# GpSimd splits three of the four blocks of each attention's output, and the projection takes them ahead of the last normalisation

## The reference

```python
xn = _ln(x, norm_s_w, norm_s_b)
spatial_out = _spatial_experts(xn, idx_s, sp_in_w, sp_in_b, sp_out_w, sp_out_b)
xt = _ln(x, norm_t_w, norm_t_b)
temporal_out = _temporal_experts(xt, idx_t, tq_w, tq_b, tk_w, tk_b, tv_w, tv_b, tp_w, tp_b)
fused = _cross_mha(spatial_out, temporal_out, cross_in_w, cross_in_b, cross_out_w, cross_out_b)
x = x + fused
h2 = _ln(x, norm_mlp_w, norm_mlp_b)
x = x + (jax.nn.gelu(h2 @ mlp_w1.T + mlp_b1, approximate=False) @ mlp_w2.T + mlp_b2)
```

## Time and profile before

| | us |
|---|---|
| median of 3 runs (lowest, highest) | 1732.79 (1730.02, 1736.64) |
| the profiled execution, its own time | 1727.27 |
| its span, first to last instruction | 1725.5 |
| PE busy | 1596.2 (93%) |
| DVE busy | 1148.8 (67%) |
| ACT busy | 879.1 (51%) |
| POOL busy | 734.6 (43%) |

### The profile page before, as it was taken

One profiled execution on the slowest core, in us unless ns is written; L12 is line 12 of the kernel. 1 busy time (PEld: TensorE's weight loads), 2 busy tenths in 40 slices (PEclk: granted clock), 3 DMA queues, 4 the chain that ended last, 5 costly groups with the idle time before them and its releaser, 6 DMA issues.

```text
span 1725.5 us, 26353 instructions
## 1 busy us (share of the span) xinstructions
PE 1596.2 (93%) x9714; PEld 1355.3 (79%) x9714; DVE 1148.8 (67%) x1810; ACT 879.1 (51%) x1733; POOL 734.6 (43%) x596
## 2 busy tenths in 40 slices
PE   2788999699999999999999998999999997899997
PEld 1567877588788888878789996878888885678876
DVE  7998826720788988840288885168888887843323
ACT  3795313320788878732177772158878873301100
POOL 3120222145446545033568744363546465532430
PEclk9999999799999999989999998999999998899999
DMA  3000021333111112042222304302111210110111
GB/s 105 13 26 2 26 66 46 111 147 72 23 39 31 31 31 61 2 184 69 60 60 61 73 7 156 85 1 52 40 31 31 55 66 19 37 38 25 49 36 59
DMA packets 37347, 91.62 MB, mean 53 GB/s; under 512 B 6457, under 2 KB 8975, under 8 KB 36712
## 3 DMA queue, kind: packets, MB, share of 16 engines
q1 hardware_dynamic: 37224, 89.99, 18.9%
HBM read 45.40 MB, written 13.86 MB: 34 GB/s over the span
## 4 chain that ended last, share of the span: by engine, by line
PE 78%; DVE 8%; ACT 5%; POOL 4%; issue 3%; DMA 2%; DVEq 1%; SPq 0%; POOLq 0%; ACTq 0%
PE ps L1000 12%; PE ps L730 12%; PE ps L731 11%; PE ps L732 11%; PE ps L981 11%; PE ps L966 7%; PE ps L967 6%; DMA w_raw<-in_weights 1%; PE ps L925 1%; PE ps L926 1%; POOL F L638 1%; PE ps L1016 1%; ACT F L1173 1%; ACT F L1260 1%; DVE F L1568 1%
## 5 line engine op out<-in xcount | busy, mean ns | idle before, releaser
L1186 ACT ACTIVATE R<-ps 125x500 fp32r<-125x500 f32 (+3 forms) x632 | 291.8, 508 | 147.0 <-PE ps L981 145.6
L583 POOL TENSOR_TENSOR w_hi<-w_raw,zero 128x512 fp32r<-128x512 f32 x92 | 110.5, 1201 | 593.0 <-PE ps L732 282.4
L1767 DVE TENSOR_REDUCE TB<-ps 125x1 f32<-125x1250 f32 (+4 forms) x240 | 299.5, 1263 | 82.9 <-PE ps L967 56.5
L1776 DVE TENSOR_TENSOR R<-ps,R 125x500 fp32r<-125x500 f32 (+3 forms) x632 | 324.1, 569 | 12.9 <-ACT R L1186 12.9
L1173 ACT ACTIVATE F<-ps,TB 125x1250 f32<-125x1250 f32 (+4 forms) x240 | 276.1, 1157 | 60.2 <-DVE TB L1767 60.2
L1000 PE MATMUL ps<-R 125*128 125x252 f32 (+1 forms) x2080 | 288.9, 286 | 2.3 <-DVE F L1819 2.3
L981 PE MATMUL ps<-ident,F 125*125 125x125 f32 x2040 | 260.1, 275 | 9.6 <-ACT F L1173 8.5
L1000 PEld LDWEIGHTS ps<-R 125*128 125x128 f32 x2080 | 256.0, 189 | 2.6 <-DVE R L1776 1.6
L981 PEld LDWEIGHTS ps<-ident,F 125*125 125x125 f32 x2040 | 239.8, 189 | 12.9 <-ACT F L1173 12.4
L966 PE MATMUL ps<-R 128*125 128x512 f32 (+5 forms) x624 | 240.5, 386 | 5.1 <-DVE R L1776 4.0
L730 PE MATMUL ps<-R,w_hi 128*128 128x512 f32 (+3 forms) x576 | 212.1, 368 | 24.4 <-POOL w_lo L598 13.9
(11 more groups left out here) (203 smaller groups left out, 2416.2 us busy)
## 6 DMA issues: line engine op xcount, KB each, us to landing
R<-F SPq DMA_DIRECT2D x96, 312.5 KB, 5.2
w_raw<-in_weights SPq DMA_DIRECT2D x88, 256.0 KB, 2.6
F<-in_weights SPq DMA_DIRECT2D x3, 1024.0 KB, 8.5
x_d<-F SPq DMA_DIRECT2D x10, 250.0 KB
zt_d<-F SPq DMA_DIRECT2D x1, 2500.0 KB, 14.0
F<-zt_d SPq DMA_DIRECT2D x1, 2500.0 KB, 9.3
xt_d<-F SPq DMA_DIRECT2D x4, 625.0 KB, 3.1
qc_d<-F SPq DMA_DIRECT2D x4, 625.0 KB, 5.7
```

Source lines behind the costliest of these rows:

```text
L583: return eng.tensor_tensor(to, a, zero[0:to.shape[0], :].to_broadcast(list(to.shape)), ALU.add)
L1186: eng.activation(probs_run(K, n, 0, part, lo, hi), ps[0:P, 3 * (n % 2) + bank, P * (lo - j0):P * (hi - j0)] .rearrange("p (c t) -> p c t", ...
L1767: ins = eng.tensor_reduce(out=ngm[0:P, 2 * (n % 2) + part:2 * (n % 2) + part + 1], in_=flat(n % 2)[0:P, at:at + P * blocks], op=ALU.max, a ...
L1776: eng.tensor_tensor(probs_run(K, n, 1, part, lo, hi), ps[0:P, 3 * (n % 2) + bank, P * (lo - j0):P * (hi - j0)] .rearrange("p (c t) -> p c ...
```

## The change

GpSimd gets a new function, `cut_outputs`, after its other work of an attention: it splits blocks 0, 1 and 2 of ZT into X1, each as soon as the buffers that lie there are no longer read and the block is normalised. For this the four buffers are laid out anew, so that the even head's lie under blocks 0 and 1. Block 3 is split by ScalarE and VectorE in the same three parts in which it is normalised (`last_lo`, semaphore `ce`). TensorE multiplies block 0 before the last `spread_inverses` (`begin_product`) and the others behind it (`continue_product`); the three parts of the last spread use three banks instead of two. In turn 2 the first four row tiles are done block by block, and the first two MLP units are split by GpSimd between the hi tiles. SP's reload of ZT waits for the new semaphore.

```diff
-        QSH = [R[:, HB:HB + 1250], R[:, HB + 1250:HB + 2500]]
-        QSL = [R[:, HB + 2500:HB + 3750], R[:, HB + 3750:HB + 5000]]
-        KS = [R[:, HB + 5000:HB + 6250], R[:, HB + 6250:HB + 7500]]
-        VS = [R[0:P, HB + 7500 + 1280 * b:HB + 8780 + 1280 * b].rearrange("p (c n) -> p c n", c=NT) for b in range(2)]
+        QSH = [R[:, HB:HB + 1250], R[:, HB + 2500:HB + 3750]]
+        QSL = [R[:, HB + 1250:HB + 2500], R[:, HB + 3750:HB + 5000]]
+        KS = [R[:, HB + 5000 + 2530 * b:HB + 6250 + 2530 * b] for b in range(2)]
+        VS = [R[0:P, HB + 6250 + 2530 * b:HB + 7530 + 2530 * b].rearrange("p (c n) -> p c n", c=NT) for b in range(2)]
...
-            eng.wait_ge(sp["os"].lo, KC)
+            eng.wait_ge(sp["os"].lo, KC - 1)
+            eng.wait_ge(ce.lo, 3)
...
+            def cut_outputs(K):
+
+                _, S = after_attention(K)
+                free = [(A.scores, K.super(7 * K.S - 1)), (A.pv, K.group(7 * K.G - 1)), (A.scores, K.super(K.N - 1))]
+                for k, (came, count) in enumerate(free):
+                    eng.wait_ge(came, count)
+                    eng.sem_inc(held, 1)
+                    eng.wait_ge(A.norm, 3 * (K.pairs0 + k + 1))
+                    hi_part(X1[0][:, k, :], ZT[:, k, :]).then_inc(S.hi, 1)
+                    eng.wait_ge(S.hi, k + 1)
+                    eng.tensor_tensor(X1[1][:, k, :], ZT[:, k, :], X1[0][:, k, :].bitcast(F32), ALU.subtract
+                                      ).then_inc(S.lo, 1)
...
                     residual_rows()
+                cut_outputs(K)
                 eng.wait_ge(A.bc, 3 * (K.pairs0 + H // 2))
...
                                   ALU.add).then_inc(sp["m"].hi, 1)
-            with eng.Fori(0, 2 * NQ) as q:
+                if i in (6, 8):
+                    cut_unit(UNIT["mlp"] + i // 2 - 3, i // 2 - 3)
+            cut_unit(UNIT["mlp"] + 2, 2)
+            cut_unit(UNIT["mlp"] + 3, 3)
+            with eng.Fori(1, 2 * NQ) as q:
...
+            def begin_product(K):
+
+                unit, S = after_attention(K)
+                eng.wait_ge(w_split, 2 * unit + 2)
+                eng.wait_ge(S.lo, 1)
+                if K.turn < 2:
+                    cols_part(K, 0, 0)
+                else:
+                    for i in range(4):
+                        rows_part(i, 0)
+
+            def continue_product(K):
+
+                unit, S = after_attention(K)
+                for k in range(1, KC):
+                    if k < KC - 1:
+                        eng.wait_ge(S.lo, k + 1)
+                    else:
+                        if K.turn == 0:
+                            eng.wait_ge(w_split, 2 * unit + 4)
+                            for k1 in range(KC - 1):
+                                cols_part(K, 1, k1)
+                        eng.wait_ge(ce.lo, 3 * K.turn + 3)
+                    if K.turn < 2:
+                        ins = cols_part(K, 0, k)
+                    else:
+                        eng.wait_ge(w_split, 2 * (unit + k) + 2)
+                        for i in range(4):
+                            ins = rows_part(i, k)
...
+                begin_product(K)
                 eng.wait_ge(A.post, K.group(H * K.G - 1))
                 for j in range(3):
-                    if j:
-                        eng.wait_ge(A.norm, 3 * (K.pairs0 + H // 2 - 1) + j - 1)
-                    spread_inverses(K, H // 2 - 1, j, 7 - j % 2)
+                    spread_inverses(K, H // 2 - 1, j, 7 - j)
+                continue_product(K)
...
+                for j in range(3):
+                    eng.wait_ge(A.norm, 3 * (K.pairs0 + H // 2 - 1) + j + 1)
+                    eng.activation(X1[0][:, KC - 1, last_block(j)], ZT[:, KC - 1, last_block(j)], ACT.Copy
+                                   ).then_inc(ce.hi, 1)
...
+                def last_lo(j):
+                    eng.wait_ge(ce.hi, 3 * K.turn + j + 1)
+                    eng.tensor_tensor(X1[1][:, KC - 1, last_block(j)], ZT[:, KC - 1, last_block(j)],
+                                      X1[0][:, KC - 1, last_block(j)].bitcast(F32), ALU.subtract).then_inc(ce.lo, 1)
                 for j in range(3):
-                    normalise(H // 2 - 1, j, 7 - j % 2)
+                    normalise(H // 2 - 1, j, 7 - j)
+                    if j:
+                        last_lo(j - 1)
+                last_lo(2)
```

More of the change, by code:

```diff
@@ L414, in gnn_ffn_program, with after_attention, last_block @@
         unit_ok, acc_ok = sem("unit_ok"), sem("acc_ok")
+        def after_attention(K):
+            return UNIT[("qo", "ut", "uc")[K.turn]], sp[("os", "ot", "oc")[K.turn]]
+        def last_block(j):
+            return slice(4 * P * j, min(T, 4 * P * j + 4 * P))
         def inverse_part(K, part):
@@ L742, in turn, with product_cols @@
                 ins.then_inc(L.tr, 1)
-            def product_cols(J, unit, X, free, n0=0, k_ready=None, k0=0, last=None, rows=None, tiles=None):
-                for m in range(4):
+            def product_cols(J, unit, X, free, n0=0, k_ready=None, k0=0, last=None, rows=None, tiles=None,
+                             begin=0):
+                for m in range(begin, 4):
                     eng.wait_ge(w_split, 2 * (unit + m) + 2)
@@ L771, in product_cols, with cols_part @@
                     ins.then_inc(w_used, 1)
-            def product_part(J, i, k, unit, X, free, n0=0, ready=None, k0=0):
-                if k == 0 and (not isinstance(n0, int) or n0 + i >= 2):
+            def cols_part(K, m, k):
+                wk = slice(128 * k, 128 * k + 128)
+                for lo, n in CHUNKS:
+                    if m == 1 and k == 0 and lo == 2 * BANK:
+                        eng.wait_ge(A.norm, 3 * (K.pairs0 + H // 2))
+                    ins = three(flat(m % 2)[:, lo:lo + n], w_hi[:, m, wk], w_lo[:, m, wk],
+                                X1[0][:, k, lo:lo + n], X1[1][:, k, lo:lo + n], k == 0, k == KC - 1)
+                return ins
@@ new lines, in rows_part @@
+            def rows_part(i, k):
+                tk = slice(P * i, P * i + P)
+                return three(ps[0:P, i, :], X1[0][:, k, tk], X1[1][:, k, tk], w_hi[:, k, :], w_lo[:, k, :],
+                             k == 0, k == KC - 1)
+            def begin_product(K):
[7 more added lines that the diff above has]
+                        rows_part(i, 0)
@@ new lines, in continue_product @@
+            def continue_product(K):
[15 more added lines that the diff above has]
+                            ins = rows_part(i, k)
+                            if k == KC - 1:
+                                ins.then_inc(pj["uc"].ps, 1)
+                if K.turn < 2:
+                    ins.then_inc(w_used, 1)
+                if K.turn == 0:
+                    cols_part(K, 1, KC - 1).then_inc(w_used, 1)
@@ L776, in product_part @@
+            def product_part(J, i, k, unit, X, free, n0=0, ready=None, k0=0, since=2):
+                if k == 0 and (not isinstance(n0, int) or n0 + i >= since):
                     eng.wait_ge(free, n0 + i - 1)
@@ L790, in product_part, with product_tile @@
                         eng.sem_inc(w_used, 1)
-            def product_tile(J, i, unit, X, free, n0=0, ready=None, k0=0):
+            def product_tile(J, i, unit, X, free, since):
                 for k in range(KC):
-                    product_part(J, i, k, unit, X, free, n0, ready, k0)
+                    product_part(J, i, k, unit, X, free, since=since)
             def product_rows(J, unit, X, free, n0=0, ready=None, k0=0, again=False, evicted=None,
@@ L1105, in _ @@
             attend(KT_)
[L1106 removed]
+            product_cols(pj["u"], UNIT["ut"], X1, pj["u"].v, begin=1)
             product_cols(pj["qk"], UNIT["kc"], X0, pj["qk"].a, n0=20, k_ready=pj["u"].t,
@@ L1111, in _ @@
             attend(KC_)
-            for i in range(NT + 2):
+            for i in range(4, NT + 4):
                 if i < NT:
-                    product_tile(pj["uc"], i, UNIT["uc"], X1, pj["uc"].v, ready=sp["oc"].lo)
-                if i >= 2:
-                    j = i - 2
+                    product_tile(pj["uc"], i, UNIT["uc"], X1, pj["uc"].v, since=6)
+                if i >= 4:
+                    j = i - 4
                     eng.wait_ge(ln3.nrm, j + 1)
```

14 lines of the change are left out of this document (3 added, 11 removed).

## The result

The changed kernel takes 1742.04 us (median of 5 runs, 1738.81 to 1747.75) against 1731.03 for the kernel before: ratio 1.0069, 95% interval 1.0053 to 1.0086. It is slower, by 9 to 15 us, and outside the range that was forecast. Its profiled execution took 1743.23 us with a span of 1741.5.

A forecast was written before the change was run, and what follows sets the result against it. TensorE, busy 93% of the span, was taken as the bound. Turns of -2.9, 0 and +3.2 gave +0.3 us on the profiled 1727.27; with the median 5.5 above, 1733.0 us was forecast, ratio 1.000, range 1724 to 1740.

The forecast's parts named there:

- First turn: End of the first attention turn: spread blocked until 734.6, next product at 765.2, a gain of 2.9 us.
- The lock: VectorE operations with two SBUF operands and GpSimd operations shut each other out; spread 3.4 us later in the first turn.
- 2.3 us for the clock: First turn: TensorE loses 2.3 us to half clock after idling 2.9 us in one piece.
- the row that I had said was missing: Rows of before showed no 2.9 us block of VectorE by GpSimd, only a piece delayed by 1.06 us.
- rival of no blocking: VectorE's pieces not blocked: first turn gains 6.2, second 4.5, third costs 2.7; 1724.8 us; chance 0.19.
- Second turn: End of the second turn: XR's load issued at 1053.6, output block 2 starts at 1064.8; gain 0.
- Third turn: End of the third turn: first `attended` at 1460.4, first MLP block ends at 1500.6; cost 3.2 us.
- VectorE's pace is its own: Third turn's tile loop: nine VectorE steps take 25.5 us, so the last `attended` comes at 1486.
- the slower rival: VectorE holds TensorE up in the first MLP quarter if the last lo tile passes 1499: 1739 to 1742 us; chance 0.16.
- The margin of 1.7 us: Third turn: last lo tile forecast at 1497.3, against the 1499 from which the slower rival decides.

The follow-up runs named there:

- xr_early: Changed kernel with SP issuing the load of XR ahead of the load of unit ut+3 in the second turn: 1740.26 us, ratio 1.0046 to the kernel before.
- third_alone: Changed kernel with the first two turns put back as before, only the third changed: 1742.42 us, ratio 1.0068 to the kernel before.
- rows_between: Changed kernel with six residual rows ahead of GpSimd's third-turn blocks, two behind unit uc+3, two behind hi tiles: 1731.40 us, ratio 0.9996 to the kernel before.
- lag_two: Changed kernel with TensorE transposing a third-turn tile two products behind its product, not four: 1742.91 us, ratio 1.0061 to the kernel before.
- first_alone: Changed kernel with the second and third turns put back as before, only the first changed: 1731.05 us, ratio 0.9997 to the kernel before.
- lo_held: Changed kernel with GpSimd's lo part of block 2 waiting for VectorE's last lo pieces of the inverses: 1736.93 us, ratio 1.0029 to the kernel before.

## Why the prediction was wrong, step by step

**First turn: mechanism right, the gain in part luck.** The lock was seen in the rows of before and priced right: spread at 734.1 for 734.6. The gain forecast as 2.9 was 2.8 in the profile, but 0 to 2.8 over all of them and 1.3 on average. The sum kept 2.3 us for the clock; it cost 1.7 in three profiles, this one among them, and 3.4 in five. The Trainium skill's rule ("SBUF — State Buffer", section "SBUF: two separate sides"), that the shared port pair is an exclusive lock for the whole instruction, is borne out by this trace: the row that I had said was missing is there, a piece of 0.42 us that takes 3.05, 2.6 of them behind GpSimd's 2.9 us operation, and for the pair in the second turn 5.72 for 1.56. The rival of no blocking is refuted. The kernels that hold the lo part show what it would have been worth: 5.3 us in the first turn against the old form, priced 6.2, and 2.0 in the second, priced 4.5, which with the load issued early is 6.1.

**Second turn: mechanism right, size off by about 2.** XR issued 1053.9 for 1053.6, output block 2 at 1065.5 for 1064.8. I took 0; this pair of traces gives 2.5, the average 1.8. The error is in taking a wait at its length: the sum had TensorE waiting for the eviction at no cost, since it was ahead anyway, and the wait cost it 1.6 us of clock behind it. `xr_early`, which has no such wait, shows none of the cost either.

**Third turn: the step that failed.** The first `attended` was right, 1461.4 for 1460.4. Wrong was the sentence "VectorE's pace is its own", 25.5 us for the nine steps. They took 30.3. VectorE's own work was priced right, 25.3, but it waited for 5.0 us (28.7 and 3.3 in the quicker profiles, such as `third_alone`): its lo tile stands behind GpSimd's hi tile, that behind ScalarE's eviction, that behind the transposes, and these behind a product four tiles further on. The sum put these waits at nothing. With the weight splits between the hi tiles, TensorE's first MLP block starts at 1497.8, not at 1490.6, and ends at 1506.1, where 1500.6 was forecast and 1497.40 stood before: 8.7 late. The last lo tile ended at 1503.7 for 1497.3, past the 1499 from which the slower rival was to decide, and the last hidden split at 1535.2 where that rival had 1533.4. TensorE's two waits for VectorE there (0.60 and 0.98) and what follows them make another 2.2, so the cost is 10.9 and not 3.2. The 7.7 between them are 1.0 at the first `attended`, 4.8 in the nine steps, 1.5 from the last one to the MLP's start (6.1 for 4.6) and the 2.2, less 1.7 for a first block that took 8.3 us and not 10.0.

**The slower rival came nearest**, with 1739 to 1742 as its time; I gave it 0.16, and ended the range at 1740, short of its own upper price. Its condition was met and TensorE did wait for VectorE in the first MLP quarter, but its way was another: it had 3.2 us lost at the first block, additions that keep their 23 us, and 5.7 more by waits; measured were 8.7, 19.1 and 2.2. That its time fits is in part luck. The margin of 1.7 us against it was smaller than what I left out, the hand-overs between engines inside one tile.

`rows_between` adds what the prediction took as given. That the residual rows end at 1436.95 and nothing in the change moves them is true; but the first tile is 13.3 us late, and four of these rows moved behind give 15.1 of it back. `lag_two` shows that a shorter lag gives at most 1.9 of the 10.9: the waits for the hi tiles go, and one of 2.6 us for TensorE comes in their place.

**What stays open:** whether the new places of the heads' buffers, which all kernels here share, cost a little. They don't cost the 5.3 us ahead of the first mark: `first_alone` takes 1731.05 where the kernel before takes 1731.18, with a gain in the first turn of 1.3 us on average, which leaves about 1 us for such a cost (none to 2 by its interval). No kernel has that edit alone. What a loop without the circle of four engines would give is open too, since `lag_two` brings a new wait.

## What to carry to other kernels

Work given to an idle engine is not free at the two places where it stands in front of something: in its own queue (here residual rows ahead of it; four of the ten moved behind gave the 11 us back) and at what it shares with its neighbour (here an operation of VectorE on the path, about 4 us in each of two turns). Both are mended by order alone: put the rows that nobody awaits behind, and hold the long operation until the short one is through. And where a stage is a loop over tiles through four engines, price a step by its circle, from one eviction to the next, and not by the busiest engine's work alone (here 25.3 us of work, and 28.7 to 30.3 with the waits).

## What the hardware showed

- VectorE's and GpSimd's subtractions from operands in SBUF shut each other out for whole operations, both ways: 0.42 became 3.05 us, 1.56 became 5.72, and GpSimd's lo part 2.86 became 3.70. With GpSimd's held back they were 0.41 and 2.87.
- A wait of TensorE of 2 to 2.5 us can cost more than its length. After 2.01 us in the second turn the clock was 0.60 for the next four; after 1.88 in `lo_held` it was 0.59. Of the 4.0 us that holding the lo part gave in the first turn, 2.6 are the earlier spread; the rest, 1.4, is of the size of what the clock had cost.
- The same wait doesn't cost the same each time: behind the same 2.5 us in the first turn the clock cost 1.7 us in three profiles and 3.4 in five.
